# An attention and mixture-of-experts layer: a rank orders each step's work on three engines, ScalarE squares more blocks, the last batch is staged tighter, and expert sums alternate between two blocks

## The chip, the cores and the metric

One core of one Trainium2 chip. The metric is the device time of one launch in microseconds, lower is better. A kernel is launched several times and its median counts.

## The reference, cut to what matters

For 16 sequences of 512 tokens with 256 features, the layer adds to x an attention part and a mixture-of-experts part, both of the layer-normed x:

```
qg, kv = split_heads(xn @ Wqg, 16), split_heads(xn @ Wkv, 16)
queries, keys, values = l2norm(qg[..., :16]), l2norm(kv[..., :16]), l2norm(kv[..., 16:])
attn = square(relu(queries @ keys^T))
aggr = attn @ values
out  = tanh_norm(aggr) * tanh(silu(gates))          # gates = qg[..., 16:]
y    = out @ Wout
...
routed = sum over the 4 chosen of 16 experts of weight * (silu(x @ g) * (x @ u)) @ d
shared = the same form with two shared experts, for all tokens
return x + y + routed + shared
```

There is no softmax: a block of scores goes through a relu and a square, and that product is the weight on the values. The tanh_norm needs the norm of a head's aggregate, so nothing of `out` can be formed before a batch's attention is complete.

## The kernel before

Every engine runs a list of operations that is worked out ahead: `at(engine, step, kind, ...)` puts an operation into a numbered step of an engine, and `order_of` (L286) writes out the steps in turn. Inside a step the operations stand in the order in which the `place_...` functions were called, `place_attention` first. The engines have no common clock; semaphores tie them together, and each engine works its own list strictly in order.

There are 512 attention steps (32 per batch, L53). A step g is one block of 128 keys for one pair of heads:

- TensorE: `scores` (L1573, tile sim, two matmuls "S") and two steps later (LAG = 2) `values` (L1586, tile av, "AV") with the values.
- ScalarE: `relu` twice (L1250, ring<-sim). ring has 4 buffers, so a relu waits for the square two steps back.
- Square: pf<-ring, on VectorE (L818) or on ScalarE (L1260). `by_act` (L110) decides: blocks n of which step n // 2 lies before 128 or after 392 go to ScalarE one in four, the others one in eight. pf has 6 buffers.
- After the fourth block of a pair, ScalarE's `take_heads` (L1284) copies av to agg and `square_heads` (L1294) squares it; TensorE sums ("N", L1600), VectorE's `head_norms` (L834, an_a<-wk) copies the sum out.

Beside it, in the same steps: the projections of the next batch (QK, V, T; tiles wk, sqr, qk_raw, vf, qkt), gates and output of the batch before (`place_after`, L157), until step 107 the layer norm and routing of all batches (`place_prep`, `place_route`, many small VectorE operations, and scatters on GpSimd), from step 132 to about 390 the 79 expert tiles (`place_tiles`; hf, hh, hl, yo), and from step 392 the sums of expert outputs (`place_sums`, L250). All matmul results but sim, av and acc share three PSUM banks, wk; a matmul group waits until the group three before it is drained.

A sum takes for one block of 128 tokens four rows of y_rows each (GpSimd `gather`, L1437, tile yg, four buffers) and adds them, weighted, one after the other to zs or y_sb (VectorE `add`, L881). The helper `Chain` makes VectorE wait for each of these results before the next operation.

`place_after` works off a finished batch: `heads` (L841) is a chain of 16 small VectorE operations with a tanh on ScalarE in it (th, L1301), WT and wt turn the weights, then for each of eight pairs t: gate (G on TensorE; silu and tanh on ScalarE, L1320 and L1322), WB (L1629, the weights spread), gated (VectorE, L865 and L869), ah (ScalarE, L1329), al (GpSimd, L1422), O (12 matmuls into acc, L1643). For the last batch the gates lie in pf and ring and wait until attention is done. `finish` (L872) scales acc and adds it to y_sb, which is stored, and loaded anew for the next batch (`store_base`, `load_residual`).

## Time and profile before

| what | value |
|---|---|
| median of 3 runs | 2572.99 us (2564.82 to 3488.87) |
| profiled execution | 2573.24 us |
| its span in the profile | 2571.4 us |
| busy: TensorE matmul, VectorE, ScalarE, GpSimd | 86%, 77%, 63%, 41% of the span |
| mean granted TensorE clock | 0.907 of full speed |

The span is what the profile covers from its first to its last instruction; 1.8 us of the execution lie outside. An engine's busy share says how long it had an instruction running, not whether others waited for it.

### The profile page before, as it was taken

The numbers are of one execution on the slowest core, as the hardware profiler recorded it, in microseconds if no ns is written. First come the engines' busy times: TensorE is split into PE (matmuls) and PEld (weight loads), VectorE is DVE, ScalarE is ACT, GpSimd is POOL, SyncE is SP. The second block draws the span as 40 slices with busy tenths as digits, with TensorE's granted clock in tenths as the row PEclk, the third lists the DMA queues.
The fourth block names the chain that finished last, engine by engine and source line by source line (L and its number), as shares of the span: only waits on it lengthen the run. The fifth ranks groups of instructions, "written<-read, shape, count | busy, mean of one in ns | idle before, by whom it ended". The sixth has DMA issues, their size and how long they took to land.

```text
span 2571.4 us, 39885 instructions
## 1 busy us (share of the span) xinstructions
PE 2213.8 (86%) x12217; PEld 1047.4 (41%) x12217; DVE 1978.8 (77%) x4013; ACT 1622.2 (63%) x2874; POOL 1043.5 (41%) x908
## 2 busy tenths in 40 slices
PE   4777687678889999999999999999999888888985
PEld 3333243234334444444444444444444433333432
DVE  6998999999986776657676566676657998998853
ACT  4545555566666667666666666676766665666752
POOL 1145466566832222122222122222123677775452
PEclk8767887798899999999999999999999988898997
DMA  3435455333453453544445343443443354452130
GB/s 111 121 122 165 121 162 174 105 115 108 135 184 85 105 124 95 124 101 122 101 105 121 99 117 98 106 115 105 111 114 95 90 150 117 117 138 78 58 77 22
DMA packets 377905, 290.34 MB, mean 113 GB/s; under 512 B 246464, under 2 KB 341312, under 8 KB 377440
## 3 DMA queue, kind: packets, MB, share of 16 engines
q1 hardware_dynamic: 353120, 220.65, 32.8%
q0 software_dynamic: 24576, 67.14, 8.3%
q8 instruction: 102, 1.67, 0.3%
q14 instruction: 107, 0.88, 0.1%
HBM read 115.75 MB, written 113.77 MB: 89 GB/s over the span
## 4 chain that ended last, share of the span: by engine, by line
PE 44%; DVE 34%; issue 12%; POOL 4%; ACT 3%; DMA 2%; DVEq 0%; ACTq 0%; POOLq 0%; SPq 0%
PE wk L1504 23%; PE av L1596 11%; DVE pf L818 8%; PE acc L1643 4%; PE sim L1583 3%; DVE zs L893 3%; PE wk L1605 2%; DVE vf L804 2%; POOL yg L1447 2%; DVE nm_t L728 2%; ACT ring L1254 2%; DVE nm_a L780 1%; DVE gate_sb L865 1%; POOL x_rows L1433 1%; DVE qkt L811 1%
## 5 line engine op out<-in xcount | busy, mean ns | idle before, releaser
L818 DVE TENSOR_TENSOR pf<-ring 128x512 f32<-128x512 f32 x834 | 629.0, 786 | 344.8 <-ACT ring L1254 336.4
L1254 ACT ACTIVATE ring<-sim 128x512 f32<-128x512 f32 x1024 | 554.3, 594 | 398.0 <-PE sim L1583 385.7
L1596 PE MATMUL av<-pf,vf 128*64 128x512 f32 x2048 | 603.6, 670 | 10.1 <-DVE pf L818 9.6
L1422 POOL TENSOR_TENSOR al<-agg,ah 128x512 f16<-128x512 f32 x128 | 160.7, 1255 | 678.5 <-ACT ah L1329 678.0
L1415 POOL TENSOR_TENSOR hl<-hf,hh 128x512 f16<-128x512 f32 x111 | 138.3, 1246 | 468.6 <-ACT hh L1275 468.5
L1447 POOL DMA_INDIRECT yg<-y_rows,at_y x256 | 267.0, 1043 | 87.0 <-issue 68.2
L1433 POOL DMA_INDIRECT x_rows<-xs,idx x256 | 266.5, 1041 | 84.0 <-issue 67.2
L1583 PE MATMUL sim<-qkt 64*128 64x512 f16 x1024 | 222.8, 407 | 40.2 <-ACT ring L1254 35.9
L1504 PE MATMUL wk<-xg,wt_t 128*128 128x512 f16 x948 | 239.4, 390 | 10.5 <-DVE qkt L811 10.5
L1583 PEld LDWEIGHTS sim<-qkt 64*128 64x128 f16 x1024 | 52.8, 93 | 455.3 <-issue 337.7
L1504 PE MATMUL wk<-wa_h,xtp 128*128 128x512 f16 (+1 forms) x1024 | 223.0, 343 | 12.5 <-issue 9.9
L1605 PE MATMUL wk<-pair_sel,sqh 128*128 128x2 f32 x1024 | 140.7, 259 | 47.5 <-DVE qkt L811 15.6
L1221 ACT ACTIVATE sqr<-wk 128x512 f32<-128x512 f32 x192 | 114.4, 596 | 101.5 <-PE wk L1504 87.6
L1596 PEld LDWEIGHTS av<-pf,vf 128*64 128x64 f32 x2048 | 107.5, 143 | 161.7 <-issue 120.5
L1643 PE MATMUL acc<-wo_h,ah 128*128 128x256 f16 x512 | 146.5, 286 | 27.5 <-POOL al L1422 27.5
L1504 PE MATMUL wk<-xtg,wa_h 128*128 128x512 f16 x512 | 157.9, 391 | 13.5 <-DVE an_a L838 11.5
L1605 PEld LDWEIGHTS wk<-pair_sel,sqh 128*128 128x128 f32 x1024 | 135.7, 204 | 77.6 <-issue 51.6
L1504 PE MATMUL wk<-wt_t,hh 128*128 128x256 f16 x632 | 133.3, 278 | 27.9 <-DVE qkt L811 14.5
L1329 ACT ACTIVATE ah<-agg 128x512 f16<-128x512 f32 x128 | 80.3, 628 | 108.8 <-DVE agg L869 108.7
L1643 PE MATMUL acc<-wo_l,ah 128*128 128x256 f16 x512 | 146.6, 286 | 0.0
L1643 PE MATMUL acc<-wo_h,al 128*128 128x256 f16 x512 | 146.5, 286 | 0.0
L1504 PEld LDWEIGHTS wk<-wa_h,xtp 128*128 128x128 f16 x1024 | 90.8, 103 | 128.6 <-issue 90.4
(228 smaller groups left out, 4089.9 us busy)
## 6 DMA issues: line engine op xcount, KB each, us to landing
y_rows<-yo SPq DMA_DIRECT2D x79, 512.0 KB, 3.3
wt_t<-w_parts SPq DMA_DIRECT2D x79, 384.0 KB, 3.4
raw_b<-w_exp SPq DMA_DIRECT2D x36, 384.0 KB, 3.7
x_rows<-xr SPq DMA_DIRECT2D x17, 512.0 KB, 4.8
x_sb<-x SPq DMA_DIRECT2D x16, 512.0 KB, 4.5
x_tok<-xr SPq DMA_DIRECT2D x16, 512.0 KB, 4.5
xs<-x_tok SPq DMA_DIRECT2D x64, 128.0 KB, 2.3
y_sb<-x SPq DMA_DIRECT2D x16, 512.0 KB, 5.2
```

The costliest lines, as they stand in the source:

```text
L818: tt(pf[:, n % NH_, :], ring[:, n % NR_, :], ring[:, n % NR_, :], ALU.mult).then_inc(pf_dve, 1)
L1221: a(sqr[n % 2][:, :], bank(*key)[:, :], ACT.Square).then_inc(rawsq_done, 1)
L1254: a(ring[:, n % NR_, :], sim[n % 2][:, :], ACT.Relu, scale=S_SCALE).then_inc(relu_done, 1)
L1415: tt(hl[:, n % 2, :], hf[:, n % 2, :], hh[:, n % 2, :], ALU.subtract).then_inc(h_lo, 1)
L1422: tt(al[:, n % 2, :], agg[:, slot(b, t), :], ah[:, n % 2, :], ALU.subtract).then_inc(a_lo, 1)
L1433: pool.indirect_dma_start(out=x_rows[:, :], out_offset=bass.IndirectOffsetOnAxis(ap=idx[:, n:n + 1], axis=0), in_=xs[:, k, :], in_offset=N ...
L1447: pool.indirect_dma_start(out=yg[m % 4][:, j, :], out_offset=None, in_=y_rows[:, :], in_offset=bass.IndirectOffsetOnAxis(ap=at_y[:, n:n + ...
L1504: ins = mm(dst, w[k], xx[k], start=first and i == 0, stop=last and i == n - 1, skip_group_check=not (first and last))
L1583: mm(sim[half][:, :], qkt[h % 2][rows, 4 + pair, j * P:(j + 1) * P], qkt[h % 2][rows, pair, :], start=True, stop=True).then_inc(sim_full, 1)
L1596: ins = mm(av[64 * half:64 * half + 64, :], vf[h % 2][:, j, hd * DV:(hd + 1) * DV], pf[:, (2 * g + half) % NH_, :], start=(j == 0), stop=( ...
L1605: ins = mm(bank("N", b, t)[:, 2 * k:2 * k + 2], sqh[:, n % 2, k * P:(k + 1) * P], pair_sel[:, :], start=True, stop=True)
L1643: ins = mm(to, w[:, blk], xx, start=(b not in opened and k % 2 == 0 and i == 0), stop=(last and k % 2 == 1 and i == 2), skip_group_check=True)
```

## The change

- `by_act`: in the first and last part of the program every second square goes to ScalarE (n = 1, 3, 5, 7 of 8), in the middle part every fourth (3 and 7 of 8).
- `order_of`: on ScalarE, VectorE and GpSimd the operations of a step are sorted by `RANK`: relu first; then take and sqh; then those that others wait for (raw, turned, silu, gate, wt, gated, hid, hn, yd, al, hl and others); then what is not named; square last. The step of each operation stays as it was. TensorE and the DMA queue aren't sorted.
- `place_after` for the last batch alone: all eight gates within steps +2 to +5, WB one per step rather than one in three, O two steps behind its WB rather than three, the second shared unit five steps earlier.
- `add`: one call per two blocks, at the place of the second; the four additions of the two blocks alternate, each waiting for the one before the last. `gather` waits until both blocks of a pair are added before it reuses their buffers.

```diff
--- before.py
+++ after.py
@@ -111,7 +111,7 @@
 
     step = n // 2
     every = 4 if step < FIRST_TILE_AT - 4 or step > FIRST_SUM_AT else 8
-    return n % every == every - 1
+    return n % 8 in ((1, 3, 5, 7) if every == 4 else (3, 7))
 
 
 def place_attention(b):
@@ -165,22 +165,26 @@
     at("dve", base + 6, "heads", b, 3)
     at("pe", base + 7, "WT", b)
     at("act", base + 7, "wt", b)
+    last = b == B - 1
     for t in range(NP_):
-        g = base + (4 + 2 * t if t < 3 else 3 * t + 1)
+        g = base + (2 + t // 2 if last else 4 + 2 * t if t < 3 else 3 * t + 1)
         at("pe", g, "G", b, t)
         at("act", g, "gate", b, t)
     for t in range(NP_):
-        w = base + 8 + 3 * t
+        w = base + 8 + (t if last else 3 * t)
         at("pe", w, "WB", b, t)
         at("dve", w, "gated", b, t)
         at("act", w + 1, "ah", b, t)
         at("pool", w + 1, "al", b, t)
-        at("pe", w + 3, "O", b, t)
+        at("pe", w + (2 if last else 3), "O", b, t)
     place_unit(("s", b, 0), base + 5, base + 6, base + 10)
-    place_unit(("s", b, 1), base + 11, base + 12, base + 16)
+    if last:
+        place_unit(("s", b, 1), base + 6, base + 7, base + 11)
+    else:
+        place_unit(("s", b, 1), base + 11, base + 12, base + 16)
     at("sp", base + 20 if b < B - 1 else base + 3, "res", b)
-    at("dve", base + 33, "fin", b)
-    at("sp", base + 34, "base", b)
+    at("dve", base + (20 if last else 33), "fin", b)
+    at("sp", base + (20 if last else 34), "base", b)
 
 
 def place_prep(c):
@@ -255,7 +259,8 @@
             at("sp", s + 6, "out", c)
         for k in range(NB):
             at("pool", s - 3 + 3 * k // 2, "gather", c, k)
-            at("dve", s + 3 * k // 2, "add", c, k)
+            if k % 2:
+                at("dve", s + 3 * k // 2, "add", c, k - 1)
 
 
 TAKE_FIRST = False
@@ -283,6 +288,12 @@
 HI = max(max(PLACED[e]) for e in PLACED)
 
 
+
+RANK = {"relu": 0, "square": 5, "take": 2, "sqh": 2}
+RANK.update({kind: 3 for kind in ("raw", "turned", "silu", "gate", "wt", "ya", "xf", "logits", "hn", "hid", "gated", "yd",
+                                  "loqk", "hl", "al")})
+
+
 def order_of(engine):
     out = []
     for step in range(LO, HI + LAG + 1):
@@ -291,7 +302,10 @@
         attends = engine == "pe" and 0 <= step - LAG < STEPS * B
         if attends and (step - LAG) % NB == NB - 1:
             out.append((step, ("AV", step - LAG)))
-        out += [(step, key) for key in PLACED[engine].get(step, [])]
+        keys = PLACED[engine].get(step, [])
+        if engine in ("act", "dve", "pool"):
+            keys = sorted(keys, key=lambda key: RANK.get(key[0], 4))
+        out += [(step, key) for key in keys]
         if attends and (step - LAG) % NB < NB - 1:
             out.append((step, ("AV", step - LAG)))
     return out
@@ -872,6 +886,8 @@
             def finish(b):
                 dve.wait_ge(out_mm, NP_ * (b + 1))
                 dve.wait_ge(res_loaded, 16 * (b + 1))
+                if b in SUM_FIRST:
+                    dve.wait_ge(add_step, NB * TOPK * (SUM_NO[b] + 1))
                 for m in range(2):
                     rows = y_sb[:, 2 * m:2 * m + 2, :]
                     v.scalar_tensor_tensor(out=rows, in0=acc[m][:, :].rearrange("p (s d) -> p s d", s=2),
@@ -880,19 +896,23 @@
 
             def add(c, k):
                 n = NB * SUM_NO[c] + k
-                dve.wait_ge(gathered[n % 4], 64 * (n // 4 + 1))
+                for m in range(2):
+                    dve.wait_ge(gathered[(n + m) % 4], 64 * ((n + m) // 4 + 1))
                 if c in SUM_FIRST:
                     dve.wait_ge(res_loaded, 16 * (c + 1))
-                    z = y_sb[:, k, :]
+                    z = y_sb
                 else:
                     dve.wait_ge(z_loaded[LATE_NO[c] % 2], 16 * (LATE_NO[c] // 2 + 1))
-                    z = zs[LATE_NO[c] % 2][:, k, :]
-                link = Chain(add_step, TOPK * n)
-                m = NB * c + k
+                    z = zs[LATE_NO[c] % 2]
+                done = TOPK * n
                 for j in range(TOPK):
-                    link(v.scalar_tensor_tensor(out=z, in0=yg[n % 4][:, j, :],
-                                                scalar=w_tok[:, TOPK * m + j:TOPK * m + j + 1], in1=z,
-                                                op0=ALU.mult, op1=ALU.add))
+                    for m in range(2):
+                        if j:
+                            dve.wait_ge(add_step, done - 1)
+                        w = TOPK * (NB * c + k + m) + j
+                        v.scalar_tensor_tensor(out=z[:, k + m, :], in0=yg[(n + m) % 4][:, j, :], scalar=w_tok[:, w:w + 1],
+                                               in1=z[:, k + m, :], op0=ALU.mult, op1=ALU.add).then_inc(add_step, 1)
+                        done += 1
 
             def route(g):
 
@@ -1441,7 +1461,7 @@
                     for i in range(2):
                         pool.wait_ge(y_stored[i], 16 * ((TILES + 1 - i) // 2))
                 if m >= 4:
-                    pool.wait_ge(add_step, TOPK * (m - 3))
+                    pool.wait_ge(add_step, 2 * TOPK * ((m - 4) // 2 + 1))
                 for j in range(TOPK):
                     n = TOPK * (NB * c + k) + j
                     pool.indirect_dma_start(
```

What stands in a row on VectorE at steps 200 and 201, in the middle part, before (pf<-ring is a square, gate_sb<- and agg<- the operation gated, hf<- hid, yo<- yd):

```order
L818 TENSOR_TENSOR pf<-ring 128x512 x2
L728 TENSOR_TENSOR nm_t<-nm_y 128x96
L729 SCALAR_TENSOR_TENSOR nm_t<-nm_a,nm_t 128x96
L730 SCALAR_TENSOR_TENSOR nm_y<-nm_t,nm_y 128x96
L796 SCALAR_TENSOR_TENSOR qk_raw<-qk_raw,nm_y 128x512
L865 TENSOR_TENSOR gate_sb<-gate_sb,wk 128x512
L869 SCALAR_TENSOR_TENSOR agg<-agg,attn_scale,gate_sb 128x512
L824 SCALAR_TENSOR_TENSOR hf<-wk,up_scale,hf 128x512
L818 TENSOR_TENSOR pf<-ring 128x512 x2
L796 SCALAR_TENSOR_TENSOR qk_raw<-qk_raw,nm_y 128x512
L804 SCALAR_TENSOR_TENSOR vf<-vf,nm_y 128x512
L831 TENSOR_SCALAR yo<-wk,out_scale 128x512
```

and now:

```order
L879 TENSOR_TENSOR gate_sb<-gate_sb,wk 128x512
L883 SCALAR_TENSOR_TENSOR agg<-agg,attn_scale,gate_sb 128x512
L838 SCALAR_TENSOR_TENSOR hf<-wk,up_scale,hf 128x512
L742 TENSOR_TENSOR nm_t<-nm_y 128x96
L743 SCALAR_TENSOR_TENSOR nm_t<-nm_a,nm_t 128x96
L744 SCALAR_TENSOR_TENSOR nm_y<-nm_t,nm_y 128x96
L810 SCALAR_TENSOR_TENSOR qk_raw<-qk_raw,nm_y 128x512
L832 TENSOR_TENSOR pf<-ring 128x512 x2
L845 TENSOR_SCALAR yo<-wk,out_scale 128x512
L810 SCALAR_TENSOR_TENSOR qk_raw<-qk_raw,nm_y 128x512
L818 SCALAR_TENSOR_TENSOR vf<-vf,nm_y 128x512
L832 TENSOR_TENSOR pf<-ring 128x512
```

The gated, hid and yd that stood behind two squares now stand ahead of them, and the squares close the step. Of the two squares of step 201 one has gone to ScalarE.

VectorE in the last part, the sums for one batch (zs<-), before:

```order
L893 SCALAR_TENSOR_TENSOR zs<-yg,w_tok,zs 128x256 x4
L818 TENSOR_TENSOR pf<-ring 128x512
L838 COPY an_a<-wk 128x4x2
L893 SCALAR_TENSOR_TENSOR zs<-yg,w_tok,zs 128x256 x4
L818 TENSOR_TENSOR pf<-ring 128x512 x3
L780 TENSOR_REDUCE nm_a<-sqr 128x32
L865 TENSOR_TENSOR gate_sb<-gate_sb,wk 128x512
L869 SCALAR_TENSOR_TENSOR agg<-agg,attn_scale,gate_sb 128x512
L893 SCALAR_TENSOR_TENSOR zs<-yg,w_tok,zs 128x256 x4
L818 TENSOR_TENSOR pf<-ring 128x512 x2
L780 TENSOR_REDUCE nm_a<-sqr 128x32
L893 SCALAR_TENSOR_TENSOR zs<-yg,w_tok,zs 128x256 x4
```

and now:

```order
L913 SCALAR_TENSOR_TENSOR zs<-yg,w_tok,zs 128x256 x8
L832 TENSOR_TENSOR pf<-ring 128x512 x2
L879 TENSOR_TENSOR gate_sb<-gate_sb,wk 128x512
L883 SCALAR_TENSOR_TENSOR agg<-agg,attn_scale,gate_sb 128x512
L794 TENSOR_REDUCE nm_a<-sqr 128x32
L832 TENSOR_TENSOR pf<-ring 128x512
L794 TENSOR_REDUCE nm_a<-sqr 128x32
L913 SCALAR_TENSOR_TENSOR zs<-yg,w_tok,zs 128x256 x8
L832 TENSOR_TENSOR pf<-ring 128x512
L852 COPY an_a<-wk 128x4x2
```

Four groups of four additions have become two groups of eight, and runs of three and two squares have become two and one.

TensorE after the end of attention, from the last gate ahead of the turned weights (id,wst) to the first spread of weights (wt,sel), before (wa_h and wa_l are gates, shw with xtg the shared units, acc with shw their output):

```order
L1504 MATMUL wk<-xtg,wa_h 128x512 x2
L1504 MATMUL wk<-xtg,shw 128x512 x6
L1623 MATMUL wk<-id,wst 32x128 x4
L1504 MATMUL wk<-xtg,wa_h 128x512 x2
L1504 MATMUL wk<-xtg,wa_l 128x512 x2
L1504 MATMUL wk<-xtg,wa_h 128x512 x2
L1629 MATMUL wk<-wt,sel 128x512
L1504 MATMUL wk<-xtg,wa_h 128x512 x2
L1504 MATMUL wk<-xtg,wa_l 128x512 x2
L1504 MATMUL wk<-xtg,wa_h 128x512 x2
L1643 MATMUL acc<-shw,hh 128x256
```

and now, up to the first output:

```order
L1524 MATMUL wk<-xtg,wa_l 128x512 x2
L1524 MATMUL wk<-xtg,wa_h 128x512 x2
L1524 MATMUL wk<-xtg,shw 128x512 x18
L1643 MATMUL wk<-id,wst 32x128 x4
L1524 MATMUL wk<-xtg,shw 128x512 x6
L1649 MATMUL wk<-wt,sel 128x512 x2
L1663 MATMUL acc<-wo_h,ah 128x256
L1663 MATMUL acc<-wo_h,al 128x256
L1663 MATMUL acc<-wo_l,ah 128x256
L1663 MATMUL acc<-wo_h,ah 128x256
```

Before, two gates and one unit stood ahead of id,wst; now all eight gates and one and a half units do. Two spreads (wt,sel x2) now stand ahead of the first output. Further on, an output before was followed by its successor's spread and then by other work:

```order
L1643 MATMUL acc<-wo_l,ah 128x256
L1629 MATMUL wk<-wt,sel 128x512
L1504 MATMUL wk<-xtg,shw 128x512 x12
L1504 MATMUL wk<-xtg,wa_h 128x512 x2
L1504 MATMUL wk<-xtg,wa_l 128x512 x2
L1504 MATMUL wk<-xtg,wa_h 128x512 x2
L1643 MATMUL acc<-wo_h,ah 128x256
L1643 MATMUL acc<-wo_h,al 128x256
```

In the new order the output of pair t is followed by the spread of pair t + 2, so a spread always runs one output ahead.

## Rows read from the trace of the kernel before

**Rows 1.** The page: busy time, share of the span and instructions of each engine

```profile
PE 2213.8 (86%) x12217; PEld 1047.4 (41%) x12217; DVE 1978.8 (77%) x4013; ACT 1622.2 (63%) x2874; POOL 1043.5 (41%) x908
```

**Rows 2.** Windows: PE, PEld, DVE, ACT, POOL busy, PEclk, DMA, GB/s; last row: L1254 alone

```profile
53.00:750.20 697.20, 530.30 (x2629) 252.74 (x2628) 647.86 (x1726) 407.26 (x721) 378.74 (x336) 0.80 0.44 138
750.20:1967.00 1216.80, 1165.63 (x6846) 557.43 (x6845) 815.19 (x1373) 828.33 (x1469) 293.41 (x223) 0.98 0.43 106
1967.00:2383.00 416.00, 351.25 (x1874) 156.48 (x1873) 371.39 (x643) 269.21 (x486) 283.27 (x264) 0.88 0.43 117
2383.00:2492.80 109.80, 98.03 (x534) 42.39 (x532) 81.27 (x148) 78.14 (x143) 50.73 (x46) 0.95 0.23 58
...
53.00:750.20 697.20, 138.35 (x257) 0.80 0.44 138
```

**Rows 3.** Waits of VectorE: window 53:750.2, then window 750.2:1967 (us, times, longest)

```profile
DVE pf L818 <- ACT ring L1254: 10.4, 8, 3.1
...
DVE pf L818 <- ACT ring L1254: 286.4, 161, 4.5
```

**Rows 4.** Waits of TensorE (PE) in window 750.2:1967

```profile
PE wk L1504 <- DVE qkt L811: 24.9, 24, 1.3
PE wk L1504 <- DVE gate_sb L865: 13.4, 8, 1.7
PE wk L1504 <- DVE an_a L838: 8.1, 8, 1.0
PE wk L1605 <- DVE yo L831: 4.7, 8, 0.6
```

**Rows 5.** Windows of L818 alone, the squares on VectorE, by stage

```profile
53.00:750.20 697.20, 146.89 (x192) 0.80 0.44 138
...
1967.00:2383.00 416.00, 118.26 (x146) 0.88 0.43 117
2383.00:2492.80 109.80, 34.54 (x47) 0.95 0.23 58
```

**Rows 6.** L818, then L1260 (squares on ScalarE): duration ns min/median/max

```profile
L818 DVE TENSOR_TENSOR pf<-ring x834: 672/690/5323, 53.7 to 2492.8; 128x512 f32<-128x512 f32 x167
...
L1260 ACT ACTIVATE pf<-ring x190: 629/630/634, 57.9 to 2493.3; 128x512 f32<-128x512 f32 x190
```

**Rows 7.** Timeline: two squares without a wait between them; four chained additions (start, us)

```profile
2491.28 1.29 DVE L818 TENSOR_TENSOR pf<-ring 128x512 f32<-128x512 f32 x2
...
2503.97 2.07 DVE L893 SCALAR_TENSOR_TENSOR y_sb<-yg,w_tok,y_sb 128x256 f32<-128x256 f32 x4 [4.15 <-DMA y_sb<-x]
```

**Rows 8.** L893, the additions: durations in ns; then their windows

```profile
L893 DVE SCALAR_TENSOR_TENSOR zs<-yg,w_tok,zs x208: 468/485/3386, 2002.4 to 2412.5; 128x256 f32<-128x256 f32 x104
...
1967.00:2383.00 416.00, 120.57 (x208) 0.88 0.43 117
2383.00:2492.80 109.80, 17.88 (x32) 0.95 0.23 58
```

**Rows 9.** Timeline of the last batch: th, first WB, one O (first matmul) to the next

```profile
2511.66 0.26 ACT L1303 ACTIVATE an_t<-an_t 128x64 f32<-128x64 f32 x1 [8.15 <-DVE an_t L851]
...
2515.99 0.60 PE L1629 MATMUL wk<-wt,sel 32*128 32x512 f16 x1
...
2533.22 0.28 PE L1643 MATMUL acc<-wo_h,ah 128*128 128x256 f16 x1 [0.88 <-POOL al L1422]
...
2538.48 0.28 PE L1643 MATMUL acc<-wo_h,ah 128*128 128x256 f16 x1 [2.06 <-POOL al L1422]
```

**Rows 10.** Timeline of the end: two of a gate's six matmuls; the final scaling

```profile
2501.07 1.06 PE L1504 MATMUL wk<-xtg,wa_h 128*128 128x512 f16 x2
...
2566.56 1.41 DVE L877 SCALAR_TENSOR_TENSOR y_sb<-acc,out_scale,y_sb 128x512 f32<-128x512 f32 x2 [4.73 <-PE acc L1643]
```

## Prediction

> **What bounds the kernel now.** I began with the page [rows 1]: TensorE is busy 86% of the span, VectorE 77%, ScalarE 63%. That reads like a TensorE kernel, but the shares are means over stages, so the next view is the windows by stage [rows 2]. I cut at the relus of steps 128, 384 and 480 (750.2, 1967 and 2383 us; the 257 relus of the first piece, two a step, are its 128 steps [rows 2]) and where the relus end (2492.8). Call the pieces A (53 to 750), B (750 to 1967), C1 (1967 to 2383), C2 (to 2492.8), and the tail after that.
>
> - A, 697.2 us: VectorE is busy 647.9 us, 93%. TensorE has 530.3 us at a granted clock of 0.80. VectorE waits for relus for only 10.4 us [rows 3]. VectorE bounds A: its 1726 instructions carry the routing, the norms and the weights.
> - B, 1216.8 us: TensorE is busy 1165.6 us, 96%, at clock 0.98; VectorE 67%, ScalarE 68%. VectorE waits 286.4 us for relus [rows 3], which is plain slack. TensorE bounds B, and the four waits that cost it 51.1 us in sum (24.9 + 13.4 + 8.1 + 4.7) are all for a PSUM bank that VectorE had still to drain [rows 4].
> - C1, 416 us: VectorE 371.4 us, 89%; TensorE 351.3, 84%, at clock 0.88; ScalarE 65%. VectorE bounds it, with less lead than in A.
> - C2, 109.8 us: TensorE 98.0 us, 89% at 0.95; VectorE 74%. No projections stand here, and TensorE leads.
> - The tail, 78.6 us to the end of the span: dependencies. One output O starts at 2533.22 and the next at 2538.48 [rows 9], 5.3 us apart, and in that time one pair walks through WB, gated, ah, al.
>
> So VectorE work counts in A and C1, hardly in B, and in the tail only the order counts.
>
> **Squares moved to ScalarE.** In A the change moves 64 squares (one in four on ScalarE becomes one in two, of 256), in B 66, in C1 and C2 61, of which 16 in C2. A square on VectorE means 146.89 / 192 = 0.765 us in A and (118.26 + 34.54) / 193 = 0.792 us in C [rows 5], against a median of 0.690 [rows 6]; the longest took 5.3 us. Two squares without a wait between them take 1.29 us together [rows 7], 0.09 less than twice the median, so neighbours overlap by that much. A removed square gives back 0.765 - 0.085 = 0.68 us in A and 0.71 in C. A: 64 x 0.68 = 43 us, with 64 x 0.60 = 38 us if only undisturbed ones went, and 64 x 0.765 = 49 as the upper bound. C1: 45 x 0.71 = 32 us. C2: 16 x 0.71 = 11 us. B: VectorE isn't the bound, nothing. ScalarE pays 0.63 us for each [rows 6], 40 us in A, which takes it from 407 to 447 us of about 654, 68%: covered. In C it goes from 347 to 386 us of some 470, 82%: covered, but thinly.
>
> The Trainium skill (Perfetto Trace Analysis, Optimizing Scalar/DVE Operations) says that offloading to ScalarE makes sense where VectorE is saturated. By it the squares moved in B bring nothing, as I have them; the sum is the same.
>
> **Additions in turn.** Four chained additions take 2.07 us [rows 7], so start to start is (2.07 - 0.485) / 3 = 0.528 us, with 0.485 the median of one [rows 8]. An alternating addition waits for the one before the last, which by then has ended, so it may overlap its neighbour as the squares do: 0.485 - 0.09 = 0.40 us. That saves 0.13 us on each of 208 additions in C1 (27 us) and 32 in C2 (4 us). Both ends: nothing, if the overlap needs instructions without any wait, and 31 us. I take the full amount, as the row of two squares is the nearest. The later place of a block (up to one step) and the later release of yg cost nothing that I can see: the gathers run on GpSimd three steps ahead.
>
> The trace's chained additions stand 0.04 us apart, end to start, and its neighbours overlap by 0.09. The Trainium skill (VectorE: DVE Perf Modes, The DRAIN you can't avoid) says that chaining operations with or without semaphores costs the same, the pipeline flush being there anyway. By it the alternation would bring nothing in the sum. Rows 7 speak against it here; it stays a rival.
>
> **The rank.** On VectorE each drain (turned, hn, yd, hid, gated) moves ahead of two squares, 1.29 us. In B that is what TensorE waits for, 51 us in sum. Against it: the squares now close a step, so hid and gated, which wait for TensorE's matmuls of that very step, hold them back, and AV wants them two steps later. A step of B is 1216.8 / 256 = 4.75 us, so there is room for about one step. Bounds: a gain of 40 us (four fifths of the waits) and a loss of 15 (a new wait of 0.06 us per step). I take a gain of 10, close to the middle of the two, since a drain early in the step and a square late pull in opposite directions. In A and C1 the order inside a step doesn't shorten a saturated engine's list: nothing, bounds as counted in the range.
>
> **Sum of C.** C1: 32 + 27 = 59 us off VectorE's 371, which leaves 312 busy of 357, 87%, while TensorE's 351 would be 98% of 357 unless its clock rises from 0.88. With a clock like that of B (0.98) those matmuls would shrink by some 5 to 10%. So C1 does not get all of it: I take 50. C2: TensorE leads, of 15 us I count 5. C: 55. Its bounds are 35 (the squares of C1 alone, and 3) and 74 (32 + 27 + 11 + 4).
>
> **The tail.** Now a spread runs one output ahead, so two walks of 5.3 us overlap: 2.65, and with hand-overs 2.9 us a pair. Before: first WB at 2515.99, last sum at 2566.56 [rows 9, 10], 50.6 us. After: first walk 5.8, seven at 2.9 makes 20.3, plus 2 us for the additions of the last two blocks: 28. Saved 22. But eight gates and one and a half units now stand on TensorE before the weights can be turned, where two gates and one unit stood, and th stands behind all eight gates on ScalarE. Two of a gate's six matmuls cover 1.06 us at the lower clock [rows 10], and pairs overlap by some 0.2, so a gate costs 3 x 0.86 = 2.6 us there, and half of that, 1.3, at the full clock. From 2497 on: eight gates and one unit half would be 12 to 23 us, so th would come at 2510 to 2521, against 2511.7 before [rows 9]. I take 4 us later. Tail: -18, bounds -8 and -27.
>
> **The sum.** A 43, B 10, C 55, tail 18: 126 us. Against the profiled execution, 2573.2 us (median 2573.0, the same), that is 2447 us. With every term at its low end (A 26, two thirds of 38; B -15; C 35; tail 8) it is 54 us, 2519; with every term at its high end (49, 40, 74, 27) it is 190 us, 2383.
>
> **The rivals.**
>
> 1. Another engine takes over in A and C. For it: TensorE in A runs at clock 0.80 and waits in many places, ScalarE in C rises to 82%, and a chain of in-order engines loses some at every hand-over. Against: VectorE's 93% leaves the others 7% only. Half of the gains of A and C: 126 - 49 = 77 us, 2496 us.
> 2. Slower: squares last. The AV of a pair's fourth block stands first in TensorE's step, and take and the next pair wait on it. If VectorE runs a step behind, each of the 128 pairs leaves TensorE idle for two squares, 1.3 us: 128 x 1.3 = 166 us lost against 126 gained, 2613 us. It decides once VectorE's lag exceeds one step (4.75 us in B). Against: TensorE waited on squares in B in none of its larger rows [rows 4]; for: VectorE is busy all the time in A.
> 3. The alternation brings nothing. 27 us less from C1 and C2 as counted, 2474 us. The page named above says so; the rows of 0.528 and 1.29 us speak against it.
> 4. The order closes TensorE's waits in B nearly wholly, and A and C reach their upper bounds: 190 us off, 2383; I put it at 2390.
>
> **How the numbers follow.** Forecast 0.55, rival 1 0.18, rival 2 0.06, rival 3 0.09, rival 4 0.12. A measurement of this kernel tells about 2% (51 us) from no change; faster by over 2% means under 2521.5. The forecast is under it but for 0.01, rival 1 with 0.13 of its 0.18, rivals 3 and 4 wholly: 0.88. Within 2%: 0.06, mostly rival 1. Slower: rival 2, 0.06. The range 2395 to 2515 holds the forecast and rivals 1 and 3 but for their edges, and leaves out most of 4 and all of 2.
>
> **What would show it.** In the trace after, the relu of step 128 should come 43 us earlier, at about 707; steps 128 to 384 should take about 1207 us, with rows 4's four waits smaller; steps 384 to 480 about 366 us; additions x8 should show 0.40 us start to start; the last WB-to-sum stretch about 28 us instead of 50.6. Wrong would be: VectorE still over 92% busy in A with no shorter A; a new wait of TensorE's av on pf of tens of us in B (rival 2); additions still 0.53 apart (rival 3); TensorE or ScalarE above 95% in C1 (rival 1); the first WB later than 10 us after that of before, counted from the last AV.

## The result and the profile after

The changed kernel takes 2459.89 us (median of 4 runs, 2453.14 to 2461.74) against 2572.99 us for the kernel before (2564.82 to 2578.72): a ratio of 0.9559, 95% interval 0.9519 to 0.9598. That is 4.4% faster. A fourth run of the kernel before took 3488.87 us and is left out of these numbers. The forecast was 2447 us, so the total came out about 0.5% from it. Its terms lay much further off, and the rest of the document is about that.

The page of the changed kernel, its busy times (compare [rows 1]) and the shares of the chain that ended last:

```profile
PE 2183.9 (89%) x12217; PEld 1041.4 (42%) x12217; DVE 1821.8 (74%) x3824; ACT 1692.6 (69%) x3063; POOL 1046.4 (43%) x908
...
PE 51%; DVE 22%; issue 11%; POOL 10%; ACT 4%; DMA 1%; DVEq 0%; ACTq 0%; POOLq 0%; SPq 0%
```

VectorE lost 157 us of busy time and ScalarE gained 70. The next view is the windows by stage, cut at the same relus as in [rows 2]; columns as there (length, busy us of PE, PEld, DVE, ACT and POOL, granted clock, DMA, GB/s). The fifth row is the tail.

```profile
51.90:727.60 675.70, 534.63 (x2627) 256.42 (x2627) 605.69 (x1660) 434.13 (x785) 380.22 (x336) 0.80 0.46 142
727.60:1893.70 1166.10, 1149.33 (x6846) 553.00 (x6844) 782.21 (x1309) 846.64 (x1534) 293.19 (x223) 1.00 0.45 111
1893.70:2290.60 396.90, 340.86 (x1874) 152.91 (x1873) 306.23 (x599) 287.41 (x531) 286.12 (x263) 0.92 0.45 123
2290.60:2400.50 109.90, 99.17 (x536) 42.66 (x535) 66.16 (x133) 84.43 (x160) 49.52 (x46) 0.94 0.23 58
2400.50:2459.20 58.70, 40.12 (x236) 22.36 (x232) 27.54 (x56) 20.98 (x35) 28.50 (x27) 0.89 0.21 63
```

Put beside rows 2, in us:

| stage | before | after | moved | forecast |
|---|---|---|---|---|
| A | 697.2 | 675.7 | -21.5 | -43 |
| B | 1216.8 | 1166.1 | -50.7 | -10 |
| C1 | 416.0 | 396.9 | -19.1 | -50 |
| C2 | 109.8 | 109.9 | 0 | -5 |
| tail | 78.6 | 58.7 | -19.9 | -18 |

With 1.1 us from what stands ahead of A the sum is 112 us. B gave back five times its term. A gave half of its own, C1 two fifths.

Waits of TensorE in B (compare [rows 4]), us in total, times, longest:

```profile
PE wk L1589 <- DVE an_a L852: 7.5, 8, 0.9
PE wk L1524 <- ACT qkt L1267: 4.8, 8, 0.6
PE wk L1524 <- DVE qkt L825: 3.5, 8, 0.4
```

Of the four waits in rows 4, 51.1 us before, only the one for qkt is left, with 3.5 us. The 7.5 us for an_a stand at another matmul group (L1589, the turned projections), which had no such wait before. TensorE in B is now busy 1149.3 of 1166.1 us at a granted clock of 1.00. The 50.7 us have two parts. TensorE's idle time fell from 51.2 to 16.8 us, which is 34.4. Its busy time fell from 1165.6 to 1149.3 us for the same 6846 matmuls, which is 16.3, and the granted clock went from 0.98 to 1.00 with it. The stage has hardly anything left to give.

VectorE's own waits in B changed their kind (compare the second row of [rows 3]):

```profile
DVE gate_sb L879 <- PE wk L1649: 128.3, 40, 8.1
DVE hf L838 <- PE wk L1524: 119.1, 63, 7.9
DVE yo L845 <- PE wk L1524: 83.2, 47, 6.3
...
DVE pf L832 <- ACT ring L1274: 5.8, 18, 0.9
```

Before, it stood 286.4 us at squares whose relus had yet to come. Now it stands at drains, ready for the bank when TensorE fills it, and by the time it reaches a square the relu has mostly ended (5.8 us of waits). That is what the sort does: without it, and with the new split, the wait for relus in B is 291.9 us (experiment 1).

The price of squares that come late is paid in the first and last parts. First the waits in A of TensorE and ScalarE on squares, then TensorE's in C1:

```profile
PE av L1616 <- DVE pf L832: 78.1, 25, 9.6
...
ACT ring L1274 <- DVE pf L832: 110.4, 44, 9.1
...
PE av L1616 <- DVE pf L832: 36.3, 17, 6.6
```

These are rival 2's waits. What they cost is asked below.

### The profile page after: what moved, and what is told of

The parts are those of the page before. It is cut to its first block, busy times and chain, and to the rows that moved or that the text cites. A ratio compares the mean times of both kernels' runs of the same rounds, so it can differ in the third digit from the quotient of the medians.

```text
span 2459.2 us, 39840 instructions
## 1 busy us (share of the span) xinstructions
PE 2183.9 (89%) x12217; PEld 1041.4 (42%) x12217; DVE 1821.8 (74%) x3824; ACT 1692.6 (69%) x3063; POOL 1046.4 (43%) x908
## 4 chain that ended last, share of the span: by engine, by line
PE 51%; DVE 22%; issue 11%; POOL 10%; ACT 4%; DMA 1%; DVEq 0%; ACTq 0%; POOLq 0%; SPq 0%
PE wk L1524 24%; PE av L1616 12%; POOL yg L1467 6%; PE acc L1663 6%; DVE pf L832 4%; PE sim L1603 3%; PE wk L1625 3%; DVE vf L818 2%; POOL al L1442 1%; ACT ring L1274 1%; DVE zs L913 1%; PE wk L1649 1%; POOL x_rows L1453 1%; DVE nm_a L794 1%; PE wk L1589 1%
## 5 line engine op out<-in xcount | busy, mean ns | idle before, releaser
L1616 PE MATMUL av<-pf,vf 128*64 128x512 f32 x2048 | 594.6, 661 | 122.2 <-DVE pf L832 121.7
L832 DVE TENSOR_TENSOR pf<-ring 128x512 f32<-128x512 f32 x645 | 509.7, 809 | 21.4 <-ACT ring L1274 16.9
L1280 ACT ACTIVATE pf<-ring 128x512 f32<-128x512 f32 x379 | 237.3, 626 | 0.5
L1603 PE MATMUL sim<-qkt 64*128 64x512 f16 x1024 | 224.6, 408 | 12.6 <-ACT ring L1274 10.0
L1524 PE MATMUL wk<-xg,wt_t 128*128 128x512 f16 x948 | 230.7, 379 | 4.8 <-ACT qkt L1267 4.8
L879 DVE TENSOR_TENSOR gate_sb<-gate_sb,wk 128x512 f32<-128x512 f32 x120 | 81.9, 683 | 184.3 <-PE wk L1649 184.2
L838 DVE SCALAR_TENSOR_TENSOR hf<-wk,up_scale,hf 128x512 f32<-128x512 f32 x111 | 83.0, 748 | 134.4 <-PE wk L1524 133.8
L1288 ACT ACTIVATE hf<-wk,inv_m 128x512 f32<-128x512 f32 x111 | 76.3, 687 | 116.7 <-PE wk L1524 116.5
L1428 POOL TENSOR_TENSOR qst<-qk_raw,qst 128x512 f16<-128x512 f32 x64 | 85.2, 1332 | 152.3 <-ACT qst L1261 151.2
```

Of the source, the lines that this page charges most:

```text
L832: tt(pf[:, n % NH_, :], ring[:, n % NR_, :], ring[:, n % NR_, :], ALU.mult).then_inc(pf_dve, 1)
L1280: a(pf[:, n % NH_, :], ring[:, n % NR_, :], ACT.Square).then_inc(pf_act, 1)
L1524: ins = mm(dst, w[k], xx[k], start=first and i == 0, stop=last and i == n - 1, skip_group_check=not (first and last))
L1603: mm(sim[half][:, :], qkt[h % 2][rows, 4 + pair, j * P:(j + 1) * P], qkt[h % 2][rows, pair, :], start=True, stop=True).then_inc(sim_full, 1)
L1616: ins = mm(av[64 * half:64 * half + 64, :], vf[h % 2][:, j, hd * DV:(hd + 1) * DV], pf[:, (2 * g + half) % NH_, :], start=(j == 0), stop=( ...
```

## The experiments

Each kernel is the changed one with a single edit, unless said otherwise, and has its own ratio to the kernel before (2570 us beside it). Stage lengths come from one profiled execution each. Stage A of seven kernels whose code for A is the same came out at 675.7 to 683.1 us, mean 679.5. So in A a difference under about 4 us says nothing, and I compare with 679.5. C1 of the four kernels whose code for C1 is the same as in the changed one came out at 396.4 to 403.2 us, and scatters as much; their mean is 399.2 and the changed kernel's own 396.9 lies low in it. Where I read C1 against 396.9 below, the difference may be 2 us too large. B is steadier: in the kernels with both the sort and the new split in B it takes 1165.7 to 1167.8 us.

### 1. No sort

```diff
-        if engine in ("act", "dve", "pool"):
+        if False:
```

> The changed kernel without the sort by rank; squares split one in two, tail and alternating additions stay. Theory R (the rank drains the PSUM banks sooner in B and makes the squares late in A and C): B goes back from 1166 to about 1215 us, A falls from 676 to about 655 and C1 from 397 to about 375, TensorE's waits of av for the VectorE squares (78 us in A, 36 in C1) fall to under 20 each; total about 2465. Rival S (the moved squares made B faster, and ScalarE's longer list made A and C fall short): B stays at 1166 to 1175, A and C1 stay within 5 us of 676 and 397.

Measured: 2502.41 us, ratio 0.9727 (0.9710 to 0.9744). Windows of A and B, then TensorE's waits in B and A:

```profile
52.40:727.00 674.60, 530.80 (x2626) 251.59 (x2626) 601.33 (x1662) 443.81 (x784) 377.01 (x336) 0.80 0.46 143
727.00:1935.20 1208.20, 1157.57 (x6846) 556.02 (x6846) 775.92 (x1309) 862.57 (x1532) 289.47 (x223) 0.99 0.44 107
...
PE wk L1524 <- DVE qkt L825: 24.9, 24, 1.3
PE wk L1524 <- DVE gate_sb L879: 13.7, 8, 1.7
...
PE av L1616 <- DVE pf L832: 6.7, 6, 2.4
```

The sort alone is worth 42 us, and all of it lies in B (1208.2 against 1166.1). TensorE's idle time there is 50.6 us without it and 16.8 with it, which is 34 us; the other 8 are busy time (1157.6 against 1149.3). And the two largest of rows 4's waits are back (24.9 and 13.7 us against 24.9 and 13.4). In A the wait of AV on squares falls from 78.1 to 6.7 us, and A is only 5 us shorter than the mean, where I had expected 21. In C1 it falls from 36.3 to 3.8 us, and C1 (398.4 us) isn't shorter at all. So rival 2's wait is real and mostly stands where TensorE would have waited for something else.

### 2. The old share of squares on ScalarE, with the sort

```diff
-    return n % 8 in ((1, 3, 5, 7) if every == 4 else (3, 7))
+    return n % every == every - 1
```

> The changed kernel with the old split of squares (one in four, one in eight in the middle). Theory R: B stays within 5 us of 1166, since its gain is the rank's; A rises from 676 by 20 to 43 us, C1 by 15 to 30, total about 2505. Rival S: B rises to about 1215 and A by less than 10.

Measured: 2516.38 us, ratio 0.9775 (0.9753 to 0.9798). Windows of A, B and C1, and AV's wait in A:

```profile
52.80:761.90 709.10, 537.31 (x2626) 253.88 (x2627) 642.86 (x1724) 407.57 (x720) 383.48 (x336) 0.79 0.44 136
761.90:1942.50 1180.60, 1154.63 (x6847) 553.99 (x6846) 840.20 (x1374) 819.62 (x1469) 304.36 (x223) 0.99 0.45 110
1942.50:2349.30 406.80, 344.31 (x1873) 152.87 (x1873) 346.01 (x644) 267.28 (x486) 297.17 (x262) 0.90 0.44 120
...
PE av L1616 <- DVE pf L832: 101.2, 36, 8.9
```

A is 709.1 us, 12 longer than before the change: where VectorE is saturated, putting its squares last costs something after all. The split gives A 709.1 - 679.5 = 30 us with the sort, and 697.2 - 674.6 = 23 us without it (experiment 1). Neither is the 43 us that I counted. In C1 the split is worth 8 to 10 us, not 32. And in B, where I had it at nothing, it is worth 14. The four kernels give B as 1216.8 us with neither edit, 1208.2 with the split alone (experiment 1), 1180.6 with the sort alone (here) and 1166.1 with both. So the sort is worth 36 us there with the old split and 42 with the new, the split 9 without the sort and 14 with it.

### 3. The sort in the middle alone

```diff
-        if engine in ("act", "dve", "pool"):
+        if engine in ("act", "dve", "pool") and 128 <= step < 390:
```

> The changed kernel with the sort only in steps 128 to 389. Theory R: B keeps 1166 us, A falls to about 655 and C1 to about 375, with av waiting little for squares in both; total about 2415, faster than the changed kernel by 1.5 to 2.5%. Rival S: no stage moves by more than 5 us, total 2455 to 2465.

Measured: 2463.83 us, ratio 0.9584 (0.9566 to 0.9603): the same as the whole change. A is 671.5 us, B 1167.4, C1 397.2, so the 20 us that I expected from each of A and C1 did not come. With experiment 1 this bounds what the sort costs in A with half of the squares on ScalarE: 5 to 8 us, little more than the scatter.

### 4. The split in B taken back

```diff
-    return n % 8 in ((1, 3, 5, 7) if every == 4 else (3, 7))
+    return n % 8 in ((1, 3, 5, 7) if every == 4 else (7,))
```

> The changed kernel with one in eight squares on ScalarE in the middle, one in two elsewhere. The old split everywhere had B at 1180.6 us against 1166.1. If the split of B itself is worth those 14 us under the rank (VectorE, waiting on TensorE's groups first, has the squares late), B is at 1178 to 1183 here and the total at about 2472. If they came from A's and C's squares at the borders, B stays at 1166 to 1169.

Measured: 2480.33 us, ratio 0.9641 (0.9617 to 0.9664). The window of B and the wait in it that grew:

```profile
730.30:1909.50 1179.20, 1153.19 (x6845) 552.85 (x6844) 838.22 (x1373) 819.55 (x1469) 304.49 (x223) 1.00 0.45 110
...
PE wk L1589 <- DVE an_a L852: 18.6, 8, 2.3
```

The edit gives VectorE back 66 squares, 64 of them in B. B is 13 us longer, as in experiment 2; the whole kernel is 20 us longer by the medians, and where the other 7 lie the one profile doesn't settle (C1 in it is 403.2 us, the top of the scatter). VectorE is busy only 71% of B, yet the 64 squares count, at 0.2 us each. The wait that grew is for an_a, a small copy that the sort has already moved ahead of the step's own squares: 18.6 us against 7.5 with the split. Squares left over from the step before would delay it, which is my reading and was not tested. The Trainium skill (Perfetto Trace Analysis, Optimizing Scalar/DVE Operations) says that offloading to ScalarE may make sense where VectorE is saturated, and I followed it for B. Here it paid without saturation. The same section speaks of engines that aren't saturated but cause bubbles on others, which fits this stage; the remedy it names there, breaking up instructions, no run here tries.

### 5. The old additions

```diff
-            if k % 2:
-                at("dve", s + 3 * k // 2, "add", c, k - 1)
+            at("dve", s + 3 * k // 2, "add", c, k)
...
-                    pool.wait_ge(add_step, 2 * TOPK * ((m - 4) // 2 + 1))
+                    pool.wait_ge(add_step, TOPK * (m - 3))
```

and in `add` the four chained additions of one block, as before the change, without the wait that the change added to `finish`.

> The changed kernel with the old additions, one block at a time, each waiting for the one before. If the alternation saves 0.12 us for each of 256 additions on a bounding VectorE, C1 rises from 397 to about 420 and C2 by some 4, total about 2487. If C1 is bound by hand-overs and not by VectorE (77% busy after the change), or if the pair's later place and its wait for two gathers cost what the overlap saves, C1 stays within 6 us.

Measured: 2459.50 us, ratio 0.9566 (0.9548 to 0.9584): no difference. C1:

```profile
1896.50:2295.50 399.00, 343.14 (x1875) 154.88 (x1874) 340.21 (x599) 286.77 (x531) 284.22 (x263) 0.92 0.45 122
```

VectorE is busy 34 us more than in the changed kernel, and C1 takes 2 us more, which is inside the scatter.

### 6. Two blocks in one call, but not in turn

```diff
-                for j in range(TOPK):
-                    for m in range(2):
+                for m in range(2):
+                    for j in range(TOPK):
                         if j:
-                            dve.wait_ge(add_step, done - 1)
+                            dve.wait_ge(add_step, done)
```

> The changed kernel with the two blocks' additions still in one call, but one block after the other, each addition waiting for the one before (no alternation). If the alternation gives VectorE back 0.12 us an addition and the merging into one later call costs about as much, which is why old additions cost no more time, then C1 rises from 397 to 410 or more and C2 with it, total 2475 or more. If C1 doesn't answer to 25 us of VectorE work at all, C1 stays within 6 us and the total at 2455 to 2463.

Measured: 2476.99 us, ratio 0.9636 (0.9613 to 0.9659). C1, then the eight additions of the last batch in the timeline, here and in the changed kernel:

```profile
1894.80:2306.90 412.10, 347.50 (x1875) 154.03 (x1874) 329.41 (x599) 286.91 (x531) 280.76 (x263) 0.91 0.45 118
...
2429.55 4.01 DVE L913 SCALAR_TENSOR_TENSOR y_sb<-yg,w_tok,y_sb 128x256 f32<-128x256 f32 x8 [3.29 <-DMA yg<-y_rows,at_y]
```

```profile
2413.71 3.31 DVE L913 SCALAR_TENSOR_TENSOR y_sb<-yg,w_tok,y_sb 128x256 f32<-128x256 f32 x8 [3.13 <-DMA yg<-y_rows,at_y]
```

In turn, eight take 3.31 us; with 0.477 the median of one, that is (3.31 - 0.477) / 7 = 0.405 us start to start, as forecast. Chained they take 4.01. The alternation by itself is worth 412.1 - 396.9 = 15 us in C1, or 17 by the medians of the whole kernels. Taken with experiment 5 (399.0 us, chained and in single blocks), putting two blocks into one later call costs 13 us. Three things are in that number and were not separated: the later place, the wait for both blocks' gathers, and the later release of the buffers. In the changed kernel VectorE stands at the additions and waits, for gathers among others. Its waits in C1:

```profile
DVE zs L913 <- DMA yg<-y_rows,at_y: 16.1, 5, 6.1
DVE zs L913 <- issue: 12.2, 6, 3.0
```

With the old additions the first of these is 4.1 us.

### 7. Half of the gathered rows

```diff
-                    dve.wait_ge(gathered[(n + m) % 4], 64 * ((n + m) // 4 + 1))
+                    dve.wait_ge(gathered[(n + m) % 4], 32 * ((n + m) // 4 + 1))
...
-                        v.scalar_tensor_tensor(out=z[:, k + m, :], in0=yg[(n + m) % 4][:, j, :], scalar=w_tok[:, w:w + 1],
+                        v.scalar_tensor_tensor(out=z[:, k + m, :], in0=yg[(n + m) % 4][:, j % 2, :], scalar=w_tok[:, w:w + 1],
...
-                for j in range(TOPK):
+                for j in range(2):
```

The last pair of lines is in `gather`. The kernel leaves out two of the four rows of each token, and the additions read the two others twice.

> Leaves out two of the four rows that GpSimd gathers for each token (the additions read the two others twice). Theory G (after the change GpSimd's list sets the pace of C1: 286 us busy and 56 us between gathers of 397): 104 gathers fewer there, 1.3 us each, so C1 falls from 397 to 365 or less. Rival V (VectorE still sets it): C1 falls by less than 8 us.

Measured: 2436.96 us, ratio 0.9469 (0.9448 to 0.9490).

### 8. Half of the additions

```diff
-                for j in range(TOPK):
+                for j in range(2):
```

in `add`, with the counts that others wait for halved. The kernel leaves out two of the four additions of each token; all gathers stay.

> Leaves out two of the four additions for each token; all gathers stay. Rival V: some 48 us less VectorE work in C1, C1 falls from 397 by 20 us or more. Theory G: C1 stays within 8 us of 397, total 2450 to 2460.

Measured: 2439.47 us, ratio 0.9477 (0.9452 to 0.9501). C1 of experiment 7, then of experiment 8:

```profile
1901.40:2286.80 385.40, 339.72 (x1874) 152.46 (x1873) 312.67 (x599) 286.46 (x530) 185.18 (x159) 0.93 0.32 91
```

```profile
1900.80:2280.60 379.80, 335.94 (x1874) 151.69 (x1875) 261.16 (x495) 286.43 (x530) 282.62 (x263) 0.94 0.49 128
```

Taking 101 us of work off GpSimd shortens C1 by 11 us; taking 45 us off VectorE, already down to 77%, shortens it by 17. Neither result is what a single bound would give (C1 at 365 us or less, or all but unchanged, in experiment 7; 20 us shorter or more, or all but unchanged, in experiment 8). Neither alone is the bound, and both matter: one us less on VectorE is worth 0.38 us here, one less on GpSimd 0.11. Two limits of this: experiment 7 halves the gathers' transfers too (91 GB/s against 123), so its 11 us aren't GpSimd's alone; and the rate of VectorE isn't a constant. The alternation (23 us off it, 15 of time) gave 0.66, the squares of experiment 2 (40 us, 10 of time) 0.25.

What the chain that ended last runs through says more than the busy shares. Its shares in C1 by line, before, in the changed kernel, and in experiment 11 below (yg is the gather; the view ends its lines after a set width):

```profile
by line: issue 16.7%; DVE zs L893 14.9%; PE wk L1504 9.7%; DVE pf L818 8.7%; PE av L1596 7.4%; POOL yg L1447 6.8%; DVE vf L804 3.5%; PE acc L1643 3.3%; DVE y_sb L893 2.6%; DMA yg<-y_rows,at_y 2.3%; PE sim L1583 2.0%; DVE gate_sb L865 1.9%; 
...
by line: POOL yg L1467 33.0%; issue 19.4%; DVE zs L913 5.7%; PE wk L1524 5.2%; PE av L1616 4.9%; POOL al L1442 4.2%; DVE pf L832 3.3%; DMA yg<-y_rows,at_y 3.3%; PE acc L1663 3.0%; DVE y_sb L913 2.1%; DVE vf L818 2.0%; POOL qst L1428 2.0%; P
...
by line: POOL yg L1467 45.9%; issue 21.0%; POOL al L1442 6.5%; DMA yg<-y_rows,at_y 3.4%; POOL qst L1428 3.2%; PE av L1616 2.8%; DVE zs L913 2.4%; PE wk L1524 2.2%; POOL kst L1428 2.1%; PE acc L1663 1.6%; POOL hl L1435 1.4%; DVE y_sb L913 1.
```

As VectorE is relieved, the gathers on GpSimd take its place: 7, 33, 46%. With half of them gone (experiment 7) the chain runs through TensorE's and VectorE's work again (20% at wk, 15% at av, 12% at the additions), and the stage is only 11 us shorter. So it looks as if in C1 a second chain lies close behind the first, whichever of the two is shortened.

### 9. Five of eight squares on ScalarE in A

```diff
-    return n % 8 in ((1, 3, 5, 7) if every == 4 else (3, 7))
+    return n % 8 in ((3, 7) if every == 8 else (1, 3, 4, 5, 7) if step < FIRST_TILE_AT else (1, 3, 5, 7))
```

> The changed kernel with five of eight squares on ScalarE in the steps before 132. If VectorE (90% busy) still bounds A and all of its relief reaches the time, 32 squares of 0.71 us take A from 676 to about 653. If, as the first 64 squares did, about half is lost to hand-overs between engines, A falls by 8 to 14 us. If ScalarE's longer list makes the relus late, A rises above 676.

Measured: 2452.45 us, ratio 0.9533 (0.9514 to 0.9551); the interval overlaps the changed kernel's. A is 669.0 us, 10 under the mean for 32 more squares.

### 10. Sort in the middle, old additions, five of eight in A and C

This takes the edits of experiments 3 and 5 together with (1, 3, 4, 5, 7) in A and C. I hoped that it would beat the changed kernel.

> Sort only in steps 128 to 389, old additions, five of eight squares on ScalarE in A and C. If the parts add up: A 664 to 669 (about 5 from the sort's absence, 11 from the squares), B 1166, C1 393 to 399, C2 105, total about 2445, 0.6% under the changed kernel. If the sort is what lets ScalarE carry five of eight, A stays at 676 to 683 and the total at 2455 to 2462.

Measured: 2469.85 us, ratio 0.9600 (0.9575 to 0.9625); no gain, by the medians a loss of 10 us. The window of A, and VectorE's wait for relus in it, which is 2.8 us in experiment 9 with the same split and the sort:

```profile
53.00:731.30 678.30, 528.74 (x2627) 252.43 (x2627) 581.80 (x1630) 463.67 (x817) 376.33 (x336) 0.82 0.46 142
...
DVE pf L831 <- ACT ring L1267: 39.2, 22, 4.3
```

Without the sort a square stands early in VectorE's step and catches the relu before it has ended. The more squares ScalarE has, the more that costs: without the sort this wait is 10.4 us with a quarter of them (before), 28.0 and 21.0 with half (experiments 1 and 3), 39.2 with five eighths. With half on ScalarE the sort costs A 5 to 8 us; with five of eight it is worth 678.3 - 669.0 = 9. What the sort is worth in A depends on the split, which single edits don't show.

### 11. Six of eight squares on ScalarE in A and C

```diff
-    return n % 8 in ((1, 3, 5, 7) if every == 4 else (3, 7))
+    return n % 8 in ((1, 2, 3, 5, 6, 7) if every == 4 else (3, 7))
```

> The changed kernel with six of eight squares on ScalarE in A and C. Each square moved so far gave A about 0.45 us (the first 64) and 0.34 us (the next 32). If the gain per square goes on falling because TensorE at its lower clock and GpSimd take over, A is at 664 to 670 and C1 at 393 to 399. If ScalarE is now the longest list (about 81% in C), C1 rises above 403. If VectorE still bounds, A falls to 655 or less.

Measured: 2432.16 us (2431.91 to 2441.11), ratio 0.9469 (0.9442 to 0.9496). This beats both kernels; its interval lies clear of the changed kernel's (0.9519 to 0.9598). Windows of A and C1, and the shares of the chain of the whole kernel:

```profile
52.90:710.30 657.40, 522.36 (x2632) 249.82 (x2631) 570.55 (x1596) 462.12 (x848) 372.95 (x336) 0.82 0.47 146
...
1876.00:2264.60 388.60, 344.06 (x1877) 154.31 (x1877) 275.74 (x555) 306.22 (x574) 287.18 (x263) 0.93 0.46 125
```

```profile
PE 41%; issue 18%; DVE 18%; POOL 15%; ACT 6%; DMA 2%; ACTq 0%; DVEq 0%; POOLq 0%; SPq 0%
```

Another 64 squares off VectorE give A 22 us more; in C1 another 44 give 8. Both are more than I expected of a gain that fades (A at 664 to 670 us, C1 at 393 to 399). ScalarE stands at 70% in A and 79% in C1, so it isn't full yet. No share beyond six of eight was tried.

### 12. The old placement of the last batch

The edit is `place_after` as before the change.

> The changed kernel with the last batch placed as before. If the tighter placement is worth what the tail shows (78.7 to 58.7 us from the last relu to the end), the tail is back at 77 to 80 us, all stages before it stay within 5 us, total about 2480. If the tail got shorter because VectorE has fewer squares and faster additions there, it stays under 65 us and the total at 2460.

Measured: 2480.69 us, ratio 0.9645 (0.9628 to 0.9662). Its tail is 80.2 us against 58.7 and 78.6 before, so the placement is worth 21 us by itself. In the changed kernel's timeline the tail reads so (start, us; compare [rows 9, 10]):

```profile
2404.84 0.59 PE L1524 MATMUL wk<-xtg,wa_l 128*128 128x512 f16 x2
...
2417.96 0.26 ACT L1323 ACTIVATE an_t<-an_t 128x64 f32<-128x64 f32 x1 [0.21 <-DVE an_t L865]
2421.63 0.60 PE L1649 MATMUL wk<-wt,sel 32*128 32x512 f16 x2
2423.61 3.93 DVE L913 SCALAR_TENSOR_TENSOR y_sb<-yg,w_tok,y_sb 128x256 f32<-128x256 f32 x8 [1.01 <-DMA yg<-y_rows,at_y]
2427.46 0.68 DVE L879 TENSOR_TENSOR pf<-pf,wk 128x512 f32<-128x512 f32 x1
2431.38 0.40 PE L1663 MATMUL acc<-wo_h,ah 128*128 128x256 f16 x1 [9.15 <-POOL al L1442]
...
2436.84 0.27 PE L1663 MATMUL acc<-wo_h,ah 128*128 128x256 f16 x1
2439.89 0.27 PE L1663 MATMUL acc<-wo_h,ah 128*128 128x256 f16 x1
2454.37 1.41 DVE L893 SCALAR_TENSOR_TENSOR y_sb<-acc,out_scale,y_sb 128x512 f32<-128x512 f32 x2 [3.47 <-PE acc L1663]
```

The two outputs shown come 3.05 us apart (2436.84 to 2439.89); all seven gaps from the first output (2431.38) to the eighth (2452.85) have a mean of 3.07, instead of 5.3, against 2.9 forecast. The first WB comes 21.1 us after the last relu (2421.63 - 2400.5); before it was 23.3 (2515.99 - 2492.7). I had added 4 us there for the eight gates. From the first WB to the last scaling it is 32.7 us, forecast 28, before 50.6. Of the missing 4.7 us, 4 stand in the fourth row: eight additions hold VectorE for 3.93 us just when the first gated wants it, and the first output comes 9.75 us after its WB where I had 5.8 for a walk. Merging the additions costs a little here too: with the old ones (experiment 5) the tail is 57.5 us, 1.2 less in one profile of each.

## Why the prediction was right in sum and wrong in its terms

**What bounds the kernel.** Right for B (TensorE) and the tail, half right for A, wrong for C1 once VectorE is relieved. VectorE at 93% of A and 89% of C1 was the busiest engine and I read that as the bound. Its busy time fell as I worked out: by 42.2 us in A (647.9 to 605.7, forecast 43) and by 65.2 in C1 (371.4 to 306.2, forecast 59). The time fell by half of that in A and three tenths in C1. Where VectorE stood idle before (49 us of A) it now stands idle for 70.

**Squares: the step that failed is "a removed square gives back 0.68 us", taken as time.** As busy time it holds (42.2 / 64 = 0.66). As time, one square gave 23 / 64 = 0.35 us without the sort and 30 / 64 = 0.47 with it, and the next 64 gave 22 / 64 = 0.35. Rival 1's size, half of the gains of A and C, is what happened, and in C1 its mechanism too: another engine took over, GpSimd with its gathers (7 to 33 to 46% of the chain), not the TensorE or ScalarE that I had named. In A no single one did. The squares' share of the chain there falls from 12.9% to 6.3 and, in experiment 11, to 2.6, while no other line but "issue" (12.6 and 14.6) goes above 6.6. In which hand-over of A the half goes stays open. Deeper buffers between relu, square and AV would test it; they weren't tried.

"B: VectorE isn't the bound, nothing" was wrong as well. The squares moved there are worth 13 to 14 us (experiments 2 and 4). They are 64, not 66 as the prediction has it; no term of its sum hangs on that.

**The rank: the term was mis-sized, 10 where the runs show 42.** The rows that I read held the answer: 51.1 us of waits, all on drains that the sort moves ahead. I took a value near the middle of a gain of 40 and a loss of 15 because late squares might hold AV up. In B they do not: none of TensorE's larger waits there is for a square, and VectorE stands idle for a third of the stage, which is the likely reason. The upper bound was too low also, since it counted only the waits. With them gone TensorE's matmuls also were busy 8 us less, at a granted clock of 1.00 instead of 0.99 (experiment 1). Rival 4, that the order closes B's waits nearly wholly, was right for B alone; the rest of it, A and C at their upper bounds, was not. Of the 50.7 us that B gave, the sort has 36 to 42 and the split the rest.

"In A and C1 the order doesn't shorten a saturated engine's list: nothing" failed in a way that depends on the split. It costs A 12 us with a quarter of the squares on ScalarE, 5 to 8 with half, and is worth 9 with five eighths; in C1 nothing was seen of it (398.4 and 397.2 us without it). That is all that was seen of rival 2. Its 78 us of waits on squares are in the trace, but taking them away brought at most 8.

**Additions: the mechanism was right, the term not.** 0.405 us start to start against 0.40 forecast, 0.528 before. The 27 us counted for C1 were about 15. What failed is the sentence that the later place of a block and the later release of yg cost nothing that I can see: together with the wait for two blocks' gathers they cost about 13, so the edit as a whole brings nothing that can be measured (experiment 5). Rival 3's outcome came true, but not for its reason. The Trainium skill (VectorE: DVE Perf Modes, The DRAIN you can't avoid) would have chained and alternating additions take the same; experiment 6 shows 4.01 us against 3.31 for eight, so the measurement decides against that here. The same section adds that a next operation which is not held starts earlier, and with that the trace agrees: the alternating additions start 0.405 us apart and last 0.477.

**C1 as a whole.** Of 50 us, 19 came. I did foresee that TensorE would limit it and that its clock would rise (0.88 to 0.92). But TensorE is busy only 86% of C1, so it was not that. I had left GpSimd out of the sum, with "the gathers run on GpSimd three steps ahead"; it is busy 72% of C1 and its gathers are a third of the chain. Experiments 7 and 8 show two engines, each well under full, which both shorten the stage when relieved, and neither by what it is relieved of.

**The tail.** -18 forecast, -20 measured, and -21 by itself. The spacing of the outputs (2.9 against 3.07) was right. Two errors of 5 to 6 us cancel. The gates did not delay the first WB: it came 2 us earlier where I had 4 later, as two of a gate's matmuls took 0.59 us where rows 10 have 1.06, and all eight gates some 11 us, the low end of what I had worked out. And the additions did delay the first output.

**The sum.** A and C came out 22 + 31 + 5 = 58 us short, B and the tail 41 + 2 = 43 us over; 1 us came from ahead of A. That the total lies 13 us from the forecast is luck of the signs. The range of 2395 to 2515 held it, though three of its four terms lay outside their own bounds: A gave 21.5 us against a lowest 26, B 51 against a highest 40, and C1 and C2 together 19 against a lowest 35. Two slips of the working change nothing: two thirds of 38 is 25, not 26, and 12 to 23 us after 2497 is 2509 to 2520.

## What to carry to other kernels

These are what one kernel showed, no more. Where one engine is over 95% busy, list its waits: here all were for a buffer that another engine with slack had yet to drain, and putting the drains ahead in that engine's list gave back 36 to 42 us of 51 us of waits. In A and C1, where VectorE was at 77 to 93% and the others above half, relieving it gave between a quarter and four fifths of the busy time taken off it, about a half in the middle; ask which engine's chain comes next, GpSimd's included. Before merging calls to gain overlap, look at what the merged call must wait for: it waits for the later of its inputs.

## What the runs showed of the hardware that was not expected

- The waits that the sort took out of B were worth more than themselves: 34 us of idle time went, and 8 us of busy time with it, as the granted clock went from 0.99 to 1.00. Another 8 us of busy time lie between the kernel before (0.98) and experiment 1 (0.99) at the same idle time (51.2 and 50.6). In B these two kernels differ only in the split of squares, so it came with the split; by what way, no run shows.
- Two chains of additions in turn overlap, though each addition carries a wait (0.405 us start to start at a duration of 0.477); a chain of one does not (0.528 at 0.485).
- Eight gates after the last relu did not slow the way to the first WB (21.1 us against 23.3). The tail's mean granted clock is 0.89, and in the kernel with the old placement, where TensorE waits more, it is 0.77:

```profile
2408.30:2488.50 80.20, 47.10 (x236) 23.69 (x232) 27.09 (x56) 20.54 (x35) 27.69 (x27) 0.77 0.15 46
```

  The same 236 matmuls took 47.1 us there and 40.1 in the changed kernel.
